# First attention of a four-layer kernel: weights split a unit ahead, products moved in TensorE's order, and ScalarE scaling one head of the last two query tiles

## The reference

```python
xn = layer_norm(x, gamma_in)
q = (xn @ Wq).reshape(b, n, HEADS, DHEAD).transpose(0, 2, 1, 3) * scale
k = (xn @ Wk).reshape(b, n, HEADS, DHEAD).transpose(0, 2, 1, 3)
v = (xn @ Wv).reshape(b, n, HEADS, DHEAD).transpose(0, 2, 1, 3)
sim = jnp.where(causal_mask, mask_value, jnp.einsum('bhid,bhjd->bhij', q, k))
attn = jax.nn.softmax(sim, axis=-1)
out = jnp.einsum('bhij,bhjd->bhid', attn, v)
adj = jnp.clip(attn + jnp.eye(n), 0.0, 1.0)
deg = jnp.sum(adj, axis=-1, keepdims=True)
feats = v
for l in range(2):
    h = feats @ gnn_w[l] + gnn_b[l]
    h = jnp.einsum('bij,bjd->bid', adj, h) / deg
    feats = jax.nn.gelu(h + feats, approximate=False)
out = out + feats @ lin_w + lin_b
return layer_norm(out @ Wo, gamma_out)
```

## Time and profile before

| | |
|---|---|
| median of 3 runs | 1946.68 us (1943.61 to 1954.76) |
| profiled execution: time, span | 1947.65 us, 1945.8 us |
| mean granted TensorE clock | 0.874 |
| PE, DVE, ACT, POOL busy | 74%, 60%, 45%, 43% of the span |
| first attention | about 31 to 1040 us of the span |

### The profile page before, as it was taken

The page is one execution under the profiler, slowest core; times in us unless marked ns, Lnnn a source line. Parts: engine busy times, 40 slices in busy tenths (PEclk is TensorE's granted clock), DMA queues, the critical chain, the costliest instruction groups (busy, mean ns, idle before and its releaser), DMA issues. The chain is left out here.

```text
span 1945.8 us, 26818 instructions
## 1 busy us (share of the span) xinstructions
PE 1446.5 (74%) x8265; PEld 935.1 (48%) x8265; DVE 1175.9 (60%) x2921; ACT 881.4 (45%) x1838; POOL 834.7 (43%) x564
## 2 busy tenths in 40 slices
PE   3788888889878888888885877975328575667776
PEld 2555555555555555555544545653325321222466
DVE  4556555565546555565555854467672479999844
ACT  2456555565545555565643622322102175545334
POOL 1455445564444445665551010000005207999535
PEclk9899999999999999999998866887558777989868
DMA  1000000000000000000000000000521212322112
GB/s 54 6 6 1 5 5 5 5 0 5 6 6 1 7 6 5 5 0 5 0 1 13 1 7 6 12 20 0 186 33 37 71 35 84 102 77 92 57 45 84
DMA packets 42464, 53.45 MB, mean 27 GB/s; under 512 B 8529, under 2 KB 29930, under 8 KB 42130
## 3 DMA queue, kind: packets, MB, share of 16 engines
q1 hardware_dynamic: 39634, 46.84, 7.9%
q0 software_dynamic: 2752, 5.65, 1.2%
HBM read 42.82 MB, written 9.26 MB: 27 GB/s over the span
## 5 line engine op out<-in xcount | busy, mean ns | idle before, releaser
L372 POOL TENSOR_TENSOR l0a_A<-l0a_A,l0a_share 128x256 f32<-128x256 f32 (+7 forms) x128 | 269.6, 2107 | 147.3 <-DVE l0a_share L929 147.0
L489 ACT ACTIVATE l0a_A<-l0a_ring,l0a_low 128x512 f32<-128x512 f32 (+3 forms) x384 | 217.6, 577 | 116.1 <-DVE l0a_low L922 74.9
L688 PE MATMUL l0a_tr<-main_ident,l0a_A 128*128 128x128 f32 x1152 | 174.3, 289 | 39.0 <-DVE l0a_E L934 22.7
L934 DVE COPY l0a_E<-l0a_tr 128x512 f32<-128x512 f32 (+1 forms) x160 | 102.0, 638 | 157.8 <-PE l0a_tr L688 157.8
L919 DVE TENSOR_REDUCE l0a_low_part<-l0a_ring 128x2 f32<-128x1024 f32 (+3 forms) x128 | 130.5, 1021 | 97.5 <-PE l0a_ring L669 90.9
L688 PEld LDWEIGHTS l0a_tr<-main_ident,l0a_A 128*128 128x128 f32 x1152 | 136.5, 148 | 79.3 <-issue 57.3
L2857 PE MATMUL mx_ysum<-mx_hst,main_ident 128*128 128x512 f32 x256 | 134.1, 658 | 41.5 <-POOL mx_hst L2976 33.7
L2991 POOL TENSOR_TENSOR mx_dBu<-mx_XI,mx_BB 128x1024 f32<-128x1024 f32 x64 | 139.5, 2207 | 50.0 <-DVE mx_DT L3031 50.0
L378 POOL TENSOR_TENSOR l0a_T<-l0a_VW,l0a_small 128x512 f32<-128x512 f32 x32 | 33.4, 1043 | 277.2 <-DVE l0a_small L952 277.2
L697 PE MATMUL l0a_agg<-l0a_E,l0a_F 128*64 128x512 f32 (+3 forms) x768 | 143.9, 504 | 2.6 <-ACT l0a_U L510 2.6
L697 PE MATMUL l0a_agg<-l0a_E,l0a_VH 128*64 128x512 f32 (+3 forms) x768 | 130.9, 489 | 13.3 <-ACT l0a_E L495 13.3
(11 more groups left out here) (507 smaller groups left out, 3519.6 us busy)
## 6 DMA issues: line engine op xcount, KB each, us to landing
mx_BB<-mx_brows SPq DMA_DIRECT2D x32, 512.0 KB, 3.6
l0a_wp<-in_wqkv SPq DMA_DIRECT2D x16, 192.0 KB
moe_rows<-moe_XR SPq DMA_DIRECT2D x2, 1032.0 KB
moe_Wg<-in_f_wg SPq DMA_DIRECT2D x8, 256.0 KB, 5.7
moe_Wu<-in_f_wu SPq DMA_DIRECT2D x8, 256.0 KB, 5.9
moe_Wd<-in_f_wd SPq DMA_DIRECT2D x8, 256.0 KB, 6.0
moe_Y<-rt_zeros SPq DMA_DIRECT2D x2, 1024.0 KB, 10.9
e_back<-moe_Y SPq DMA_DIRECT2D x8, 256.0 KB, 5.1
```

The lines of the kernel that those rows point to most:

```text
L372: pool.tensor_tensor(a, a, spread(share[:, it, :], [P, 2, w]), ALU.mult).then_inc(shared, 1)
L489: act.activation(A[:, it % 3, h, c0:c0 + n], pair(k % 2)[:, h, 0:n], ACT.Exp, bias=low[:, it, h:h + 1], accum_out=s).then_inc(exp_done, 1)
L688: mm = pe.transpose(tr[n % 2][:, at:at + P], A[:, it % 3, h, t * P:(t + 1) * P], ident[:, :])
L934: dve.tensor_copy(dst, src).then_inc(turned_dve, 1)
```

## The change

Nothing of the computation is changed, only who does it and when. (1) **Weights.** weights_hi(u + 1) moves from ScalarE's body start into the scores before it, between turn_out(8) and the exponentials of piece 10; weights_lo(u + 1) moves on GpSimd to behind shares(u, 6), ahead of out2 and shares(u, 7). The load runs one unit further. (2) **Shares.** For tiles 6 and 7 GpSimd scales head 0 only; ScalarE scales head 1 with a Copy whose scale is a column (second_share). (3) **ScalarE's order.** keep_gl(0) and (1), keep_u2(1) move back; turn_out(10) moves from before the exponentials of pieces 10 and 11 to behind them and behind second_share(7). (4) **TensorE's order.** second, mix, product2 move to other score pieces; turn(11) moves to the next body behind attend(g, 0); values(u, 0) goes ahead of attend(g, 1). (5) **VectorE's order.** own_share and own_factors of half 0 move to the body's start, ahead of turn_out(11), which moves there too; set_own(1) moves behind row_low 0 and 1; out2 moves back. (6) **GpSimd's order.** shares 4 to 7 move relative to out_sum and out2.

```diff
@@ SyncE
-                if b < NB - 1:
-                    weights(slice(0, P), PAIRS * (b + 1))
+                weights(slice(0, P), PAIRS * (b + 1))
@@ GpSimd, shares
-                a = A[:, it % 3, :, 0:w]
-                pool.tensor_tensor(a, a, spread(share[:, it, :], [P, 2, w]), ALU.mult).then_inc(shared, 1)
+                heads = 2 if it < ST - 2 else 1
+                a = A[:, it % 3, 0:heads, 0:w]
+                pool.tensor_tensor(a, a, spread(share[:, it, 0:heads], [P, heads, w]), ALU.mult).then_inc(shared, 1)
@@ GpSimd, body
-                if more:
-                    weights_lo(u)
                 own_part(g, 0)
                 own_part(g, 1)
...
                     keep_vb(u, 1)
+                    shares(u, 4)
                 if third:
                     out_sum(g, prev, 0)
                 if more:
-                    shares(u, 4)
+                    shares(u, 5)
                 if third:
                     out_sum(g, prev, 1)
+                if more:
+                    shares(u, 6)
+                    weights_lo(u + 1)
                 out2(g, 0)
                 if more:
-                    shares(u, 5)
+                    shares(u, 7)
                 out2(g, 1)
-                if more:
-                    shares(u, 6)
-                    shares(u, 7)
@@ ScalarE
+            def second_share(u, it):
+                act.wait_ge(share_done, u * ST + (it + 1))
+                a = A[:, it % 3, 1, 0:(it + 1) * P]
+                act.activation(a, a, ACT.Copy, scale=share[:, it, 1:2]).then_inc(shared_act, 1)
@@ ScalarE, scores
-                if third:
-                    keep_gl(g, 0)
-                if more:
                     turn_out(u, 0)
                     exps(u, 4)
                     exps(u, 5)
-                if third:
-                    keep_gl(g, 1)
-                if more:
                     turn_out(u, 2)
                     exps(u, 6)
                     exps(u, 7)
+                if third:
+                    keep_gl(g, 0)
+                if more:
                     turn_out(u, 4)
-                if second:
-                    keep_u2(g, 1)
-                if more:
                     turn_out(u, 6)
                     exps(u, 8)
                     exps(u, 9)
+                if second:
+                    keep_u2(g, 1)
+                if third:
+                    keep_gl(g, 1)
+                if more:
                     turn_out(u, 8)
-                    turn_out(u, 10)
+                    weights_hi(u + 1)
+                    second_share(u, 6)
                     exps(u, 10)
                     exps(u, 11)
+                    second_share(u, 7)
+                    turn_out(u, 10)
@@ ScalarE, body
                 if more:
-                    weights_hi(u)
                     keep_comp(u)
@@ TensorE, turn
                     pe.wait_ge(shared, u * ST + (it + 1))
+                    if it >= ST - 2:
+                        pe.wait_ge(shared_act, u * 2 + (it - (ST - 3)))
@@ TensorE, scores: the new order, in a body of the middle
+ score 0, 1; second(0; 0-3); score 2, 3; turn 0, 1; second(1; 0, 1); score 4, 5; turn 2, 3; second(1; 2, 3, 4);
+ score 6; second(1; 5); score 7; mix(0); turn 4, 5; second(1; 6); score 8, 9; second(1; 7); turn 6; mix(1);
+ turn 7, 8; score 10, 11; product2(0); turn 9, 10; product2(1)
@@ TensorE, body
                 attend(g, 0)
+                turn(g, 11)
...
-                turn(g, 14, 15)
+                turn(g, 14, 15, 16, 17)
                 product1(g, 0)
-                turn(g, 16, 17, 18, 19)
+                turn(g, 18, 19)
+                if more:
+                    values(u, nb, 0)
                 attend(g, 1)
-                if more:
-                    values(u, nb, 0)
+                if third:
+                    turn_f(g, 0)
                 product1(g, 1)
                 if third:
-                    turn_f(g, 0)
                     turn_f(g, 1)
@@ VectorE, scores
                     row_low(u, 0, 1)
+                if second:
+                    set_own(g, 1)
...
                     row_low(u, 11)
+                if second:
+                    out2(g, 0)
+                if more:
                     turn_out(u, 9)
-                    turn_out(u, 11)
                     row_share(u, 7)
+                if second:
+                    out2(g, 1)
@@ VectorE, body
                     composite_lo(u)
+                own_share(g, 0)
+                own_factors(g, 0)
+                turn_out(g, 11)
                 turn_out(g, 13)
```

More of the change, by code:

```diff
@@ L414, in first @@
                 keep_vb(0, 1)
-                for it in range(ST):
+                for it in range(ST - 1):
                     shares(0, it)
+                weights_lo(1)
+                shares(0, ST - 1)
             def body(g, prev, nb):
                 u, more, third = g + 1, nb is not None, prev is not None
-                if more:
-                    weights_lo(u)
                 own_part(g, 0)
@@ L539, in scores @@
                     exps(u, 3)
+                    turn_out(u, 0)
+                    exps(u, 4)
+                    exps(u, 5)
+                    turn_out(u, 2)
+                    exps(u, 6)
+                    exps(u, 7)
                 if third:
@@ L542, in scores @@
                 if more:
-                    turn_out(u, 0)
-                    exps(u, 4)
-                    exps(u, 5)
+                    turn_out(u, 4)
+                    turn_out(u, 6)
+                    exps(u, 8)
+                    exps(u, 9)
+                if second:
+                    keep_u2(g, 1)
                 if third:
@@ L602, in body @@
                     keep_ft(g, 0)
-                    keep_ft(g, 1)
                 if more:
                     keep_v(u, 1)
+                if third:
+                    keep_ft(g, 1)
                 gelu1(g, 1)
@@ L778, in scores @@
                     score(u, 2, 3)
+                    turn(u, 0, 1, prev=prev)
+                if two:
+                    second(g, 1, 0, 1)
+                if more:
+                    score(u, 4, 5)
+                    turn(u, 2, 3)
+                if two:
+                    second(g, 1, 2, 3, 4)
+                if more:
+                    score(u, 6)
+                if two:
+                    second(g, 1, 5)
+                if more:
+                    score(u, 7)
                 if three:
@@ L782, in scores @@
                 if more:
-                    turn(u, 0, 1, prev=prev)
+                    turn(u, 4, 5)
                 if two:
-                    second(g, 1, 0)
+                    second(g, 1, 6)
                 if more:
-                    score(u, 4, 5)
+                    score(u, 8, 9)
+                if two:
+                    second(g, 1, 7)
+                if more:
+                    turn(u, 6)
                 if three:
@@ L790, in scores @@
                 if more:
-                    turn(u, 2, 3)
+                    turn(u, 7, 8)
+                    score(u, 10, 11)
                 if two:
-                    second(g, 1, 1, 2, 3)
-                if more:
-                    score(u, 6)
-                if two:
-                    second(g, 1, 4)
-                if more:
[L799 to L802, removed]
                     product2(g, prev, 0)
                 if more:
-                    score(u, 8, 9)
-                    turn(u, 6, 7, 8)
+                    turn(u, 9, 10)
                 if two:
                     product2(g, prev, 1)
-                if more:
-                    score(u, 10, 11)
-                    turn(u, 9, 10, 11)
             def first():
@@ L867, in tail @@
                 pe.wait_ge(turned_act, n * NK + 6 if more else n * NK)
-                pe.wait_ge(turned_dve, n * NK + 6 if more else n * NK)
+                pe.wait_ge(turned_dve, n * NK + 5 if more else n * NK)
                 pe.wait_ge(ot_kept, n * 2 - 2)
@@ L993, in scores @@
                     turn_out(u, 5)
-                if second:
-                    out2(g, 0)
-                if more:
                     row_low(u, 8)
@@ L1000, in scores @@
                     turn_out(u, 7)
-                if second:
-                    out2(g, 1)
-                if more:
                     row_low(u, 10)
@@ L1028, in body @@
                 turn_out(g, 19)
-                own_share(g, 0)
-                own_factors(g, 0)
+                own_share(g, 1)
+                own_factors(g, 1)
                 out1(g, 0)
                 set_own(g, 0)
-                own_share(g, 1)
-                own_factors(g, 1)
                 out1(g, 1)
-                set_own(g, 1)
                 scores(u if more else None, g)
```

12 lines of the change are left out of this document (3 added, 9 removed).

## The result

The changed kernel takes 1937.55 us (median of 9 runs, 1934.04 to 1938.88) against 1946.68 (9 runs, 1940.12 to 1954.76): ratio 0.9947, interval 0.993 to 0.9965, 9 us or 0.5% faster. The forecast was 1921, 26 us faster, with a range up to 1944. The sign and the place of the two main waits were right; the gain was not half of what was forecast.

A forecast was written before the change was run, and what follows sets the result against it. TensorE was taken as the bound: 49.3 us work, 8.8 waits, 1.6 slower clock a turn. 2.07 less a turn, times 12 = 24.8, plus 1.1 at the ends: 1947.65 - 25.9 = 1921.7, median 1921; range 1900 to 1944.

The forecast's parts named there:

- The scaling copies: ScalarE's two second_share copies for tiles 6 and 7, ahead of turn_out(10): taken at 2.0 us together.
- B: Stretch of a turn from score(0) to the exponentials of piece 8: 25.05 us before, forecast 23.3.
- A: Stretch of a turn from composite to score(0): 26.4 us before in a clean turn, forecast 22.7.
- The wait at turn(1): In stretch B, PE waits about 1.0 us for GpSimd's scaling of tile 1, of which 0.5 is regained.
- C: Stretch from the exponentials of piece 8 to the next composite, summed from ScalarE's list: 6.6 us before, forecast 10.3.
- A clean turn: One loop turn, composite to composite, at full clock: A, B and C sum to 56.3 us against 58.07.
- Each us more on the list of C is a us on the turn: Rival (d), slower: ScalarE's chain ahead of composite sets the turn; 1957 us or more, chance 0.06.
- the clock: Slower TensorE clock after waits: 1.6 us a turn on average before, taken at 1.3 after the change.
- Rival (b): Clock falls each turn, for longer, in attend(g, 0) behind the wait: 2.6 us a turn, 1936 us; chance 0.12.
- the ends: First composite 3.5 us later, change of sequence even, last body 4.6 less: together a gain of 1.1 us.
- The last body has no composite to wait for, 4.6 less: In the loop's last body, no composite waits for turn_out(10): 4.6 us saved.
- The change of sequence: Where the loop changes sequence: gains 3.2 us up to its tail, then gives it back through turn_out(11) behind own_share.

The follow-up runs named there:

- w1: Changed kernel with only its weights part undone (weights_hi and weights_lo back at the body's start): ratio 0.9929 to the kernel before, 1963.31 us.
- p2: Changed kernel without ScalarE's two scaling copies, GpSimd scaling both heads of tiles 6 and 7: ratio 1.0064 to the kernel before, 1959.27 us.
- p6: Kernel before with the weights ahead, plus turn_out(10) moved behind the exponentials of pieces 10 and 11: ratio 0.9879 to the kernel before, 1954.67 us.
- d1: Changed kernel with two extra ScalarE copies of 512 elements between second_share(7) and turn_out(10): ratio 1.006 to the kernel before, 1987.39 us.
- e0: Changed kernel with only VectorE's turn_out(11) moved to the head of its body, ahead of own_share: ratio 0.9929 to the kernel before, 1962.09 us.
- e2: Changed kernel with turn_out(10) between exponentials 10 and 11 and turn_out(11) at the head of VectorE's body: ratio 0.9576 to the kernel before, 1867.52 us.
- q1: The e2 kernel without ScalarE's scaling copies, GpSimd scaling both heads of tiles 6 and 7: ratio 0.9891 to the kernel before, 1955.19 us.
- p1: Kernel before with only the weights rounded and split one unit ahead: ratio 0.9608 to the kernel before, 1874.49 us.
- e1: Changed kernel with turn_out(10) moved between the exponentials of pieces 10 and 11: ratio 0.987 to the kernel before, 1925.9 us.
- e3: The e2 kernel with TensorE's turn(1) moved behind second(1; 0, 1): ratio 0.9529 to the kernel before, 1883.62 us.
- e3_again: The same kernel as e3, measured again on another chip: ratio 0.9525 to the kernel before, 1883.13 us.

## Why the prediction was wrong

**The first steps were right.** The wait for the weights went, and nearly the same length of wait came back at the composite behind turn_out(10): forecast 3.5, measured 3.13. The scaling copies, taken at 2.0, are 1.08 + 1.15. B was 23.3 and is 23.78. A was 22.7 at the full clock; it is 23.98, of which 1.7 is attend at 1.2 GHz, so 22.3. The wait at turn(1) is 0.96. C was forecast at 10.3 and is 10.36. A clean turn by these is 56.4, and the one turn without a fall of the clock took 56.46; forecast 56.3.

**C came out in part by luck.** I had added up ScalarE's list from piece 8 to turn_out(10). Its first half doesn't set the time: the exponentials of piece 10 start 5.37 or 5.38 us behind those of piece 8 in the changed kernel, without weights_hi (w1), without second_share(6) (p2) and in p6, since they wait for VectorE's reduction of piece 10. My terms up to there (2.45, 1.8, 0.53 and 0.92, less some overlap) come to nearly the same length. "Each us more on the list of C is a us on the turn" is shown only for what stands behind the exponentials of piece 11 (p2, d1).

**Mis-sized a little: the clock.** I took 1.3 a turn. It fell in eleven of the twelve turns, as it had in the kernel before (I had counted ten there; the first, 58.6, fell too), and a fall costs about 1.65. The mean is 57.90 - 56.46 = 1.44. With the clean turn's 0.16 the mean turn is 57.90 and not 57.6, 3.5 us over twelve turns. Rival (b) had the kind right, a fall in attend behind the wait, and its price, 2.6, too high.

**Failed: the ends.** "The last body has no composite to wait for, 4.6 less" is the step that failed. From the last composite to the next stage the changed kernel takes 127.60 us and the kernel before 127.49: 0.1 more. The last attend does start 3.2 us earlier in the turn, but what comes behind takes 72.8 instead of 69.5 us. Between the two attends it is 15.5 instead of 9.0: 3.5 more of idle time, above all the 3.96 at turn(13), and 3.0 more of PE's own time, 0.5 of it turn(11) and the rest the slower clock (0.78 in this stretch); behind the second attend 3.2 comes back. I had costed turn_out(11) behind own_share only with project(q) as its cover. The last body has no project, own_share starts late (behind out2) and is stretched by GpSimd, so the cover is gone. With turn_out(11) moved ahead (e0) 2.1 of the 3.3 come back; the rest is open. In e2 the last body is as long as in the changed kernel, with waits of 0.97 and 1.91 between its attends and clock 0.76 there, the longer one at turn_out(13), which still stands behind own_share.

The change of sequence came out 1.8 longer and not even. In e0 it is 2.4 shorter than in the changed kernel, so this too is turn_out(11) behind own_share. First composite: 3.7 later, forecast 3.5. Together the ends lose 5.6 where I had a gain of 1.1.

**Around the stage.** Up to the start of the next stage the changed kernel's profile is 15.6 us ahead (1042.13 against 1057.77), of 25.9 forecast; 3.5 and 6.7 of the gap are the two points above. Behind it the profiled execution lost 2.1, where nothing was changed. The last 4.5 lie between profiled executions and medians: the one before was 1.0 above its median, the one after 3.5 below. I had carried over only the 1.0, though the three runs of the kernel before spanned 1943.61 to 1954.76.

**What the sum did not ask.** Each part was priced as it stood in the whole. What the weights alone would give, and how much of it the move of one copy takes away, could have been read from my own A and C (3.7 of wait gone, 3.5 come back) and was not said.

## What to carry to other kernels

In a list kept full by hand, an edit that removes a wait and edits that add work ahead of another wait can cancel: time the parts one by one, since here one part gave 75 us, the whole 9, and undoing that part in the whole changed nothing that could be measured. Before adding up an engine's list, look for the place in it that waits for another engine: what stands ahead of it may be free (0.5 and 1.08 us here), what stands behind it is not (1.15 and 1.18). See which copy frees the buffer that the bottleneck writes next, and let it never stand behind work that waits for another engine. A wait of TensorE of 2.04 us cost 3.7 where the clock fell with it, in eleven turns of twelve, so price a wait of that size with its clock.

## What the runs showed of the hardware

**A VectorE operation with two SBUF inputs waits for the end of GpSimd's instruction.** own_share's operation takes 0.28 us alone, 3.67 beside a GpSimd instruction of 3.66 and 1.37 beside one of 1.34; in the changed kernel 1.94 beside 1.90 and 1.34 beside 1.32. In q1 one that starts 1.24 us into a GpSimd instruction of 3.60 takes 2.50. The Trainium skill says so ("SBUF — State Buffer", section "Who interferes with whom"): a VectorE instruction with two SBUF inputs and a GpSimd instruction that reads SBUF share an interface, and the later one is blocked until the other is done. The trace agrees, and I had not weighed it: moving own_share to where GpSimd is busy is what that rule speaks against. That GpSimd's own durations hardly change (3.60 and 3.66 for the same shape) fits its having started first.

**The clock fell with a wait of 2.0 to 3.1 us in a turn, nearly always.** It did in eleven turns of twelve of the changed kernel (3.1) and of p6 (2.0) and in all twelve of e1 (2.5, at another place), each of them at 0.97 or below; it stayed at 1.00 in all twelve of p1, whose longest wait is 1.4. The wait's length alone does not decide it: the clean turn of the kernel before had a wait of 3.7 at clock 1.00, the two clean turns of the changed kernel and p6 start behind waits of 2.69 and 2.05, and behind the same 2.65 ahead of the first composite the first turn of e3's kernel fell in one execution (e3_again) and not in the other (e3_turn1_later). What does decide it no run here shows.
